# A fused tokenizer, attention and mixture-of-experts layer on one core: the last attention turn reordered, the first weight split on the vector engine, and one transpose per half group's maxima

## The reference, cut to what matters

```
h = concat([tok(x), txt], axis=1)                      # 8 x 384 x 256
# attention: 16 heads of 16, latent keys and values, causal softmax
n = layernorm(h);  c = n @ W_DKV                       # latent, 64
q, k, v = n @ W_UQ, c @ W_UK, c @ W_UV
h = h + softmax(causal(q k^T / 4)) v @ W_O
# experts: 8 of them, top 2, capacity 384 tokens each, first come first served per choice
n = layernorm(h);  s = softmax(n @ router_w);  w, e = top_k(s, 2)
for k in 0, 1:                                         # (choice, expert) = one unit
    y = gelu(xe @ w1[e]) @ w2[e]                       # xe: the rows sent to expert e, 384 x 256
    out[token] += w[:, k] * y
h = h + out + bias
```

## Time and profile before

| what | value |
| --- | --- |
| median of 3 runs | 673.88 us (670.34 to 673.93) |
| the profiled execution's own time | 673.71 us |
| its span, first to last instruction | 671.9 us |
| mean granted TensorE clock | 0.974 of 2.4 GHz |
| busy: TensorE, VectorE, ScalarE, GpSimd | 617.8, 403.1, 378.0, 389.8 us |
| instructions | 13720 |

### The profile page before, as it was taken

The page is one execution under the profiler, slowest core; times in us unless marked ns, Lnnn a source line. Parts: engine busy times, 40 slices in busy tenths (PEclk is TensorE's granted clock), DMA queues, the critical chain, the costliest instruction groups (busy, mean ns, idle before and its releaser), DMA issues.

```text
span 671.9 us, 13720 instructions
## 1 busy us (share of the span) xinstructions
PE 617.8 (92%) x5082; PEld 512.7 (76%) x5082; DVE 403.1 (60%) x942; ACT 378.0 (56%) x818; POOL 389.8 (58%) x600
## 2 busy tenths in 40 slices
PE   2698999999999999999879799999999999999992
PEld 2465566676666666666559699999999999999992
DVE  4778688788998888678446244544444444444320
ACT  4347786777776776666551355455445555455440
POOL 3303232424645555464655579998888888888223
PEclk9988999999999999999978799999999999999997
DMA  6527566633534232360111743554444444442123
GB/s 225 156 57 185 177 198 179 179 101 97 158 81 119 61 106 82 95 213 28 50 48 40 222 159 67 145 128 101 89 94 95 98 108 111 108 107 48 19 23 39
DMA packets 66604, 73.86 MB, mean 110 GB/s; under 512 B 6312, under 2 KB 61586, under 8 KB 66536
## 3 DMA queue, kind: packets, MB, share of 16 engines
q1 hardware_dynamic: 56232, 59.45, 29.7%
q0 software_dynamic: 9504, 13.00, 11.2%
q10 hardware_dynamic: 800, 0.52, 0.3%
HBM read 31.62 MB, written 22.48 MB: 81 GB/s over the span
## 4 chain that ended last, share of the span: by engine, by line
PE 82%; ACT 4%; DMA 4%; issue 3%; DVE 2%; SPq 1%; POOL 1%; ACTq 0%; another core or an unknown queue 0%; DVEq 0%; POOLq 0%
PE t_bank L1764 20%; PE bank L1779 14%; PE s_bank L1779 7%; PE bank L684 7%; PE t_bank L649 6%; PE s_bank L627 5%; PE t_bank L742 3%; PE s_bank L628 3%; PE t_bank L712 2%; PE s_bank L1749 2%; PE bank L696 2%; PE bank L754 1%; PE t_bank L727 1%; PE bank L775 1%; PE t_bank L747 1%
## 5 line engine op out<-in xcount | busy, mean ns | idle before, releaser
L1726 DVE TENSOR_TENSOR hl<-h,hh 128x384 fp32r<-128x384 f32 x128 | 108.1, 852 | 152.2 <-ACT h L1689 152.2
L550 POOL TENSOR_SCALAR_AFFINE_SELECT pt<-pt 128x256 f32<-128x256 f32 x192 | 83.9, 443 | 158.3 <-ACT pt L959 121.2
L1178 DVE TENSOR_REDUCE mx<-s_bank 128x2 f32<-128x256 f32 (+2 forms) x192 | 123.1, 683 | 47.7 <-PE s_bank L628 47.2
L1686 ACT ACTIVATE hh<-t_bank 128x384 fp32r<-128x384 f32 x128 | 63.0, 492 | 134.5 <-PE t_bank L1764 132.2
L1639 POOL DMA_INDIRECT out<-yo,xr x48 | 75.4, 1570 | 57.3 <-ACT yo L1697 47.3
L959 ACT ACTIVATE pt<-t_bank 128x512 f32<-128x512 f32 x128 | 76.0, 601 | 36.6 <-PE t_bank L649 34.8
L1626 POOL TENSOR_TENSOR wl<-wr,wh 128x256 fp32r<-128x256 f32 x112 | 95.2, 884 | 1.2
L1764 PE MATMUL t_bank<-xh,wh 128*128 128x384 f32 x256 | 87.2, 341 | 0.6 <-issue 0.6
L1764 PE MATMUL t_bank<-xl,wh 128*128 128x384 f32 x256 | 86.5, 338 | 0.0
L1764 PE MATMUL t_bank<-xh,wl 128*128 128x384 f32 x256 | 86.4, 338 | 0.0
L627 PE MATMUL s_bank<-ks,qs 96*128 96x128 bf16 (+2 forms) x384 | 80.2, 278 | 3.0 <-DMA qs<-part 2.8
(11 more groups left out here) (191 smaller groups left out, 1338.3 us busy)
## 6 DMA issues: line engine op xcount, KB each, us to landing
wr<-in_w SPq DMA_DIRECT2D x16, 1024.0 KB, 5.9
qs<-part SPq DMA_DIRECT2D x96, 96.0 KB, 2.2
ks<-part SPq DMA_DIRECT2D x90, 96.0 KB, 2.2
slot_rows<-empty SPq DMA_DIRECT2D x4, 1560.0 KB, 8.9
xr<-slot_rows SPq DMA_DIRECT2D x16, 390.0 KB, 3.3
wr<-in_x SPq DMA_DIRECT2D x8, 768.0 KB, 5.5
out<-hid SPq DMA_DIRECT2D x8, 384.0 KB
qs<-mT ACTq DMA_DIRECT2D x64, 3.0 KB
```

What stands on the lines that cost most here:

```text
L550: pool.affine_select(out=blocks, in_=blocks, compare_op=ALU.is_ge, fill=0.0, base=0, pattern=[[0, 2], [1, P]], channel_multiplier=-1).then ...
L1178: ins = dve.tensor_reduce(mx[:, p // 2, j, 2 * (p % 2):2 * (p % 2) + 2], pair_region(s_bank, j), AX_X, ALU.max)
L1726: dve.tensor_tensor(hl[:, f, :], h[f % 2][:, :], hh[:, f, :].bitcast(F32), ALU.subtract).then_inc(hl_done, 1)
```

## The change

- `maxima` on TensorE: the order of `mx`, `ms` and `mT` is changed so that one transpose of 24 columns (part, head, tile) replaces the three. ACT copies 24 x 128 instead of 8 x 384. Each of the two DMAs reads 12 partitions of 128 values instead of 4 of 384. The two DMAs of turn 15's second half group are issued by SP, the others by ACT as before.
- TensorE's list for turn 15 and the tail has another order. Before: contexts_back(14, 1), project(6, 0), ranks(5), then pair 2's groups. After: pair 2's groups and `values` follow at once, project(6, 0), ranks(5) and project(6, 1) stand among and behind pair 3's groups, project(7) comes ahead of rows_back(6), and there are more and longer fillers (6, 12, 6, 12, 24, 8, 24, 230 where 30, 20, 200 stood).
- ACT's list: contexts_out(14) after all exponentials, contexts_out(15) and `early_high` (now only w2) ahead of rows_back(6).
- VectorE's list: `weigh(5)` ahead, then a half of `early_first` (a copy to the high part and the subtraction for the low part of w1), the normalise of turn 15's first half group, the other half of `early_first`, and then residual and norm of entry 6. normalise(15, 1) ahead of the row scaling of entry 6. `early_low` and `late_bias` are gone from the end; the bias adds stand behind steps 1, 3 and 5 of the first expert unit.
- SP: the weights of expert 1 are loaded ahead of the stores of entries 5 to 7.

```
-    mx = buf("mx", [P, NG, NT, GH])
-    ms = buf("ms", [P, NG, NT, MPARTS, GH], BF16)
-    mT = buf("mT", [MPARTS * GH, NG, T], BF16)
+    mx = buf("mx", [P, NG, GH, NT])
+    ms = buf("ms", [P, NG, MPARTS, GH, NT], BF16)
+    mT = buf("mT", [MPARTS * GH * NT, NG, P], BF16)
...
+    def max_rows(queue, n, grp):
+        queue.wait_ge(mT_sb, NG * n + grp + 1)
+        for a in range(MPARTS):
+            queue.dma_start(qs[(n // 2) % 2][n % 2][MROW + a:MROW + a + 1, grp * GH:(grp + 1) * GH, :],
+                          mT[a * GH * NT:(a + 1) * GH * NT, grp, :]).then_inc(m_in[grp], 16)
...
+        max_rows(sp, END, 1)
...
-            for j in range(NT):
-                mm = pe.transpose(M_b[0:MPARTS * GH, j * P:(j + 1) * P],
-                                  ms[:, grp, j, :, :].rearrange("p a h -> p (a h)"), ident_b[:, :])
-            mm.then_inc(mT_ps, 1)
+            pe.transpose(M_b[0:MPARTS * GH * NT, 0:P], ms[:, grp, :, :, :].rearrange("p a h j -> p (a h j)"),
+                         ident_b[:, :]).then_inc(mT_ps, 1)
...
         contexts_back(END - 1, 1, False)
-        project(B - 2, 0)
-        ranks(B - 3)
         shifted_scores(END, 2, 0)
         shifted_scores(END, 2, 1)
         values(END, 0)
+        shifted_scores(END, 2, 2)
         contexts_out(END - 1, 0)
-        shifted_scores(END, 2, 2)
-        project(B - 2, 1)
         shifted_scores(END, 3, 0)
         contexts_back(END, 0, False)
         shifted_scores(END, 3, 1)
+        project(B - 2, 0)
         shifted_scores(END, 3, 2)
+        ranks(B - 3)
+        project(B - 2, 1)
         values(END, 1)
+        turning(6)
         contexts_back(END, 1, False)
+        turning(12)
+        contexts_out(END, 0)
+        turning(6)
+        for k in range(2):
+            project(B - 1, k)
         for c in range(KC):
             rows_back(B - 2, c)
-        contexts_out(END, 0)
-        for k in range(2):
-            project(B - 1, k)
+        turning(12)
         router(B - 2)
-        turning(30)
+        turning(24)
         for c in range(KC):
             rows_back(B - 1, c)
         ranks(B - 2)
+        turning(8)
         router(B - 1)
-        turning(20)
+        turning(24)
         ranks(B - 1)
-        turning(200)
+        turning(230)
...
-            act.activation(mT[:, grp, :], M_b[0:MPARTS * GH, 0:T], ACT.Copy).then_inc(mT_sb, 1)
+            act.activation(mT[:, grp, :], M_b[0:MPARTS * GH * NT, 0:P], ACT.Copy).then_inc(mT_sb, 1)
...
         exps(END, 0, 1)
-        max_rows(END, 1)
...
         contexts(END, 0)
-        contexts_out(END - 1, 0)
         exps(END, 2, 2)
         exps(END, 3, 0)
         exps(END, 3, 1)
         exps(END, 3, 2)
+        contexts_out(END - 1, 0)
         contexts(END, 1)
+        contexts_out(END, 0)
+        early_high(act)
         for c in range(KC):
             rows_back(B - 2, c)
-        contexts_out(END, 0)
-        early_high(act)
...
         reciprocals(END - 1, 1)
         normalise(END - 1, 1)
+        weigh(B - 3)
+        dve.wait_ge(t_ready, 12 * END)
+        early_first(dve, 0)
+        reciprocals(END, 0)
+        normalise(END, 0)
+        early_first(dve, 1)
         residual(B - 2, 0)
         norms2(B - 2, (0, 1))
-        weigh(B - 3)
-        reciprocals(END, 0)
-        normalise(END, 0)
         residual(B - 2, 1)
         norms2(B - 2, (2,))
         variances2(B - 2)
         keep_ranks(B - 3)
         place(B - 3)
-        scaled2(B - 2)
         reciprocals(END, 1)
         normalise(END, 1)
+        scaled2(B - 2)
...
-        early_low(dve)
-        for b in range(LATE, B):
-            late_bias(b)
...
+    BIAS_AT = (1, 3, 5)
...
         for u in range(1, NX):
             load_rows(u)
-        stores(sp)
         for i in range(2):
             load_weights(1, i)
+        stores(sp)
...
     def early_high(act):
 
-        for i in range(2):
-            act.wait_ge(w_in[i], 16)
-            for half in range(2):
-                cols = slice(half * NW // 2, (half + 1) * NW // 2)
-                act.activation(wh[i][0][:, cols], wr[i][:, cols], ACT.Copy).then_inc(w_first[i], 1)
-
-    def early_low(dve):
+        act.wait_ge(w_in[1], 16)
         for half in range(2):
             cols = slice(half * NW // 2, (half + 1) * NW // 2)
-            dve.wait_ge(w_first[0], half + 1)
-            dve.tensor_tensor(wl[0][0][:, cols], wr[0][:, cols], wh[0][0][:, cols].bitcast(F32),
-                              ALU.subtract).then_inc(w_split[0], 1)
+            act.activation(wh[1][0][:, cols], wr[1][:, cols], ACT.Copy).then_inc(w_first[1], 1)
+
+    def early_first(dve, half):
+
+        cols = slice(half * NW // 2, (half + 1) * NW // 2)
+        dve.wait_ge(w_in[0], 16)
+        dve.tensor_copy(wh[0][0][:, cols], wr[0][:, cols]).then_inc(w_first[0], 1)
+        dve.wait_ge(w_first[0], half + 1)
+        dve.tensor_tensor(wl[0][0][:, cols], wr[0][:, cols], wh[0][0][:, cols].bitcast(F32),
+                          ALU.subtract).then_inc(w_split[0], 1)
...
             hidden(0, f)
             if f == SECOND_AT:
                 rows(1)
+            if f in BIAS_AT:
+                biases(dve, BIAS_AT.index(f))
```

More of the change, by code:

```diff
@@ L74 @@
 NMAT = MAT_WO + KC * DIM + KC * E
-Programs = namedtuple("Programs", "sync gpsimd tensor scalar vector early_high early_low stores", defaults=(None,) * 3)
+Programs = namedtuple("Programs", "sync gpsimd tensor scalar vector early_high early_first stores biases", defaults=(None,) * 4)
 def rows_to_all(ap, n):
@@ L139, in _ @@
         def _(dve):
-            before.vector(dve, behind.early_low)
-            behind.vector(dve)
+            before.vector(dve, behind.early_first)
+            behind.vector(dve, before.biases)
 def front(nc, common, lent, wr, w_in, routed, x, txt, params, mats, w1, w2, slot_rows, out):
@@ L965, in maxima @@
                 act.wait_ge(m_in[grp], 16 * MPARTS * n)
-            act.activation(mT[:, grp, :], M_b[0:MPARTS * GH, 0:T], ACT.Copy).then_inc(mT_sb, 1)
-        def max_rows(n, grp):
-            act.wait_ge(mT_sb, NG * n + grp + 1)
-            for a in range(MPARTS):
-                act.dma_start(qs[(n // 2) % 2][n % 2][MROW + a:MROW + a + 1, grp * GH:(grp + 1) * GH, :],
-                              mT[a * GH:(a + 1) * GH, grp, :]).then_inc(m_in[grp], 16)
+            act.activation(mT[:, grp, :], M_b[0:MPARTS * GH * NT, 0:P], ACT.Copy).then_inc(mT_sb, 1)
         def contexts(n, grp):
@@ L1087, in scalar @@
                 if p == 0 and cur:
-                    max_rows(n, 1)
+                    max_rows(act, n, 1)
                 if p == 2 and nxt:
-                    max_rows(n + 1, 0)
+                    max_rows(act, n + 1, 0)
                 if not odd and p == 0 and live(b + 2) and n:
@@ L1163, in scalar, with late_bias, vector @@
         gates(B - 1)
-    def vector(dve, early_low):
+    def late_bias(dve, b):
+        dve.wait_ge(row_done, (NT + 1) * b + NT + 1)
+        dve.tensor_tensor(hid[:, b, :, :], hid[:, b, :, :],
+                          bias.rearrange("p (o d) -> p o d", o=1).to_broadcast([P, NT, DIM]),
+                          ALU.add).then_inc(res_last, 1)
+    def vector(dve, early_first):
         steps = [0]
@@ L1177, in maxima @@
             for j in BANK_TILES[grp]:
-                ins = dve.tensor_reduce(mx[:, p // 2, j, 2 * (p % 2):2 * (p % 2) + 2], pair_region(s_bank, j),
+                ins = dve.tensor_reduce(mx[:, p // 2, 2 * (p % 2):2 * (p % 2) + 2, j], pair_region(s_bank, j),
                                         AX_X, ALU.max)
@@ L1186, in split_high @@
                 dve.wait_ge(mT_ps, G - 1)
-            dve.tensor_copy(ms[:, grp, :, 0, :], mx[:, grp, :, :]).then_inc(m_part, 1)
+            dve.tensor_copy(ms[:, grp, 0, :, :], mx[:, grp, :, :]).then_inc(m_part, 1)
         def split_low(n, grp):
             dve.wait_ge(m_part, MPARTS * (NG * n + grp) + 1)
-            dve.tensor_tensor(ms[:, grp, :, 1, :], mx[:, grp, :, :], ms[:, grp, :, 0, :],
+            dve.tensor_tensor(ms[:, grp, 1, :, :], mx[:, grp, :, :], ms[:, grp, 0, :, :],
                               ALU.subtract).then_inc(m_part, 1)
@@ L1363, in keys @@
             dve.tensor_copy(part[k][stage][:, :], bank_of(part_key(b, k))[:, 0:T]).then_inc(part_dve, 1)
-        def late_bias(b):
-            dve.wait_ge(row_done, (NT + 1) * b + NT + 1)
-            dve.tensor_tensor(hid[:, b, :, :], hid[:, b, :, :],
-                              bias.rearrange("p (o d) -> p o d", o=1).to_broadcast([P, NT, DIM]),
-                              ALU.add).then_inc(res_last, 1)
         dve.wait_ge(prm_in, 16)
@@ L1499, in vector, with biases @@
         place(B - 1)
-        early_low(dve)
-        for b in range(LATE, B):
-            late_bias(b)
-    return Programs(sync, gpsimd, tensor, scalar, vector, stores=stores)
+    def biases(dve, b):
+        late_bias(dve, LATE + b)
+    return Programs(sync, gpsimd, tensor, scalar, vector, stores=stores, biases=biases)
 def s_region(bank, j, i):
```

(4 more changed lines are left out.)

## The result

The changed kernel takes 680.74 us (median of 8 runs, 678.07 to 682.34), the kernel before took 673.71 beside it (8 runs). The ratio is 1.0104, with a 95% interval of 1.0081 to 1.0126: slower by 1.0%, where 1.4% faster was forecast. The profiled execution took 682.34 us, span 680.6, at a mean granted clock of 0.967.

What follows compares the result with a forecast made beforehand. TensorE was taken to bound the steady attention turns and expert stage, a chain over all engines the stretch between. Terms: -3.5 - 2.3 + 0 - 1.8 - 1.9 + 0.2 = -9.3, so 673.7 becomes 664.4 us; range 659.8 to 669.0.

Steps and rivals of the forecast that it cites:

- Term 1: Attention turns: one transpose per half group instead of three, 32 half groups, -3.5 us (bounds -1.8 and -4.5).
- rival of late rows: Attention turns: maxima rows' DMA lands late, delaying each of 32 landings by 0.5 us; 680 us, chance 0.02.
- the transposes hide: Attention turns: dispatch around the transposes sets the pace, so they save only 0.5 us; 667.4 us, chance 0.05.
- Term 2: Last attention turn: new order starts values earlier and has the last rows transposed sooner, -2.3 us (bounds -0.8 and -3.7).
- the clock falls: TensorE's clock drops in the last turn or in the gap before the experts; 668.1 us, chance 0.17.
- Term 3: Ranks of the last batch: VectorE's remote wait stays, 0 us; bounds -1.7 and some 0.5 slower from low-clock fillers.
- Term 4: Last batch's sends: without VectorE's work beside them they shorten, so the row load starts earlier, -1.8 us.
- Term 5: Start of expert stage: 230 fillers nearly fill the wait, clock stays at 2.4 GHz, -1.9 us (bounds 0 and -2.6).
- Term 6: First expert unit: moved bias adds and later stores are covered by VectorE's idle time, +0.2 us (bound +1.5).
- the list of what would make it wrong: Signs, among them VectorE or ACT waits in the first expert unit idling TensorE, and waits for expert 1's split weights.

Runs made afterwards that it cites:

- h3: The change again, unedited, on a chip where the kernel before took 671.52 us: 679.01 us, ratio 1.0128.
- e1: The change with 110 instead of 230 products in its last filler: 670.78 us, ratio 0.9962 to the kernel before.
- e2: The change with its bias adds back at the end of VectorE's attention program: 672.58 us, ratio 0.9991 to the kernel before.
- e5: The change with 108 long fp32 instructions (0.22 us each) as last filler instead of 230 short products: 681.39 us, ratio 1.0112 to the kernel before.
- e6: The change without its last filler: 665.96 us, ratio 0.9886 to the kernel before.
- e7: The kernel before with the one transpose and one DMA for both maxima rows of a half group: 667.27 us, ratio 0.9916.
- h2: The kernel before with one transpose and one DMA for both maxima rows, repeated on another chip: 666.96 us, ratio 0.9918.
- e3: The kernel before with the one transpose alone, still two DMAs: 671.60 us, ratio 0.9959.
- g1: The change, unedited, on a chip where the kernel before took 661.95 us: 660.42 us, ratio 0.9964.
- g2: The kernel before, unedited, profiled on a chip where it took 661.95 us: 660.89 us, ratio 0.9984.
- e4: The kernel before with 230 instead of 200 products in its last filler: 674.09 us, ratio 1.0017.
- g3: The change without its last filler, on a chip where the kernel before took 661.95 us: 661.41 us, ratio 0.9975.
- h1: The change with 50 long products as last filler, bias adds moved, one maxima DMA, one projection reordered; kernel before 671.52 us: 664.51 us, ratio 0.9883.

## Why the prediction was wrong

**Term 1, −3.5: the mechanism was right, half the size.** The stretch from the 3rd to the 29th values holds 26 of the 32 half groups, so 2.9 us were due. On the 672 chips the six profiles with one transpose and two DMAs that keep the change's order (change, h3, e1, e2, e5, e6) lie between 238.2 and 239.6, against 240.2 and 240.3: about 1.4 less. With one DMA it is 237.8 and 237.9: 2.4 less. The step that failed is "with one wait of 0.2 us seen, I cost it at nothing". The transfer did cost nothing (one wait of 0.2 us, as before); its issue on ACT did not. A half group's two issues cost ACT 0.28 us more and its copy 0.21 us less. With half of the issues the kernel gained (e7 and h2: 0.9916 and 0.9918 against 0.9959 for e3), so ACT's time for issues is paid for there; that the 0.14 us alone are the missing half of term 1 is not shown, as e7 and h2 take away more than that. The rival of late rows fell. On the 660 chips the steady turns take 236.4 to 237.1 with any of the variants, so there term 1 is zero within what the profiles can tell. That is the rival "the transposes hide", for those chips.

**Term 2, −2.3: gave about nothing.** 29th values to last ranks: 39.6 and 39.0 before, 40.0 and 39.1 after, and 36.3 and 36.0 on the 660 chip. "The values start at about 331.5, 1.6 us earlier" can't be seen in the change's own profile: counted from the 29th values, the 31st start 14.0 us later in it and 13.9 before, and the last 20.1 and 20.2. The granted clock was low there from 322.3 to 329.1, which is half of the rival "the clock falls". But such a time differs from profile to profile by more than this term. In the six 672 profiles with the change's order the 31st come 12.3 to 14.0 us after the 29th, in the five with the old order 13.9 to 15.8; the means are 1.6 us apart, so this step held on the average. The step that failed is what follows them: from the end of the last values to the transposes of the last rows I had 12.2 us in the new order. In g1 it is 12.1, as worked out, but on that chip the old order needs only 10.1 (g2), so of the 2.3 us by which the last values ended earlier after the 29th, 2.0 were lost again behind them. In the profiles of the result it was 12.9 in the new order, 11.8 in the old. POOL was not late: the deviation was ready at 348.0, and VectorE then took up its logits at 348.14 after waiting 2.75 us for router 6. "What is late next is POOL's queue of sends, no longer TensorE" was wrong: it was TensorE.

**Term 3, 0: about right for the wait, not for the fillers.** The wait was 1.50 us against 1.71. It was 0.66 to 1.73 us in all twelve profiles on 672 chips and at most 0.31 in the eight on 660 chips, with either order, so it goes with the kind of chip. What I had kept as the bound on the other side, fillers at the low clock that hold up the last ranks by 0.5 us, came true: from the last rows' transposes to the last ranks it took 5.6 us instead of 5.0, and the 24 fillers between them 2.72 us. On the 660 chip it was 5.0 in both orders.

**Term 4, −1.8: right for the sends.** First to third send ended 3.53 us after the start of the first, where it was 5.39: −1.86. Both sides were seen on the 660 chip too: the old kernel has sends of 1.65, 1.70 and 1.44 us beside VectorE's weight split and bias adds, the new one 0.97. SP issues the row load at 364.21, not 371.03. That is 1.5 us more than the sends gave: the issue follows the end of the third send after 1.44 us, where it was 2.97. It is 1.4 us in e3 and e7 too, with the old order and the long sends, and 2.97 in e4, so this part is not from the shorter sends; I had not looked at it. By the rule of the Trainium skill (SBUF — State Buffer, Who interferes with whom) that a two-input `tensor_tensor` leaves descriptor writing alone, which the page marks as inferred, this would have been 0; the rows disagree.

**Term 5, −1.9: its second half was right, its first was the error.** From the transposes to the first result product the experts took 10.9 us, 2.2 less than before. What failed is "14.0 us are filled by 230, 13.1 to 13.6 us: a gap of about 0.5 to 1", on both sides. The 14.0 us were 11.8: e6 has the rows at 367.95, and the filler starts at 356.20. So 230 products would have held the experts up by 1.3 us even at their pace of 13.00 us (g1), and on the 660 chip they did: 13.1 us from the last ranks to the experts with the filler (g1), 11.1 without (g3). There it cost nothing in the end (660.42 us with the filler, 661.41 without), as without it the clock was low for 14 us. And on the 672 chip they did not keep that pace: it took 23.3 us from their start to the experts', which is 11.6 us behind the rows. A filler in front of a wait had been priced at its pace, with no price for its running over; taking it out gave 14.8 us, to 0.9886, which is 7.7 us under the kernel before on its chip.

**Term 6, +0.2: mis-sized through term 5.** The cover I named, VectorE's idle time in the first unit, was there only while GpSimd was not splitting weights. The loads of expert 1 did not wait for TensorE, so the splits came 14.9 us after the experts' start before, 11.0 in g1 and 2.7 in the change. Beside them a bias add took 1.49 instead of 0.90 us and `hl` 1.05 instead of 0.56, and TensorE waited 3.31 us and fell to the low clock (393.9 to 400.8). e2 prices it: 301.1 down to 294.8, so 6.3 us, or 4.6 against h3; in e2 the splits also begin 2.4 us later after the experts' start, so a part of this may be theirs. The text had put the danger into the list of what would make it wrong, but not into the range.

**The rivals.** None of them came out as a whole. The one on the slower side (DMA landing late) was the wrong mechanism; the right one, a filler that ends after the rows, was within sight: it needed only the question what happens if the 0.5 to 1 us of slack is not there.

**What the gaps are stays open.** Shown: on 672 chips they came in all five profiles in which the short products ran further than 1.5 us beyond SP's issue of the first row load (the change, e1, e2, e4, h3), and not in e3, e7 and h2, whose 200 products ended 1.3 to 1.5 us after it; they begin after 85, 89, 114, 173 and 217 products (e1, h3, the change, e2, e4); short products show them and long ones do not (e5, h1). The timeline of SP beside them, over two windows:

```profile
364.21 9.05 SPq L1597 DMA_DIRECT2D xr<-slot_rows  x4
```

```profile
364.21 0.39 SPq L1597 DMA_DIRECT2D xr<-slot_rows  x1
```

The first row is four issues of 0.37 to 0.49 us merged into one, not one issue of 9 us. Behind the first of them the program has SP wait for GpSimd's last six sends, and issues the other three from 371.83 on. The end of the gaps goes with the end of that wait: 372.15 in the change, 369.0 in h3 (SP goes on at 368.80), 372.7 in e2 (372.98), 373.7 in e4 (373.79). Their start goes with nothing that I found. It lies 1.1 to 1.4 us ahead of the first issue in the change, h3 and e1, so that issue can't have begun them there, and 1.0 to 1.2 us behind it in e2 and e4. The last packet of instructions that the traces show before the gaps starts 1.5 to 6.3 us ahead of them, which is no fixed distance either.

Nor is TensorE alone late in this stretch. In e3 its transposes ended at 371.64, but ACT, which had nothing else to do, took up their first half, ready before that, at 373.81:

```profile
370.30 1.34 PE L1747 MATMUL s_bank<-ident,xr 128*128 128x128 f32 x6 [2.65 <-DMA xr<-slot_rows]
...
373.81 0.87 ACT L1679 ACTIVATE xh<-s_bank 128x384 fp32r<-128x384 f32 x2 [17.59 <-remote]
```

From the start of the transposes to that copy it took 3.51 us here, 2.06 in e7 and 1.65 in h1, and 0.54 in the change and in g1, where the transposes came after the stretch or on a 660 chip. With VectorE's wait for the ranks (term 3) that makes three engines that are late on the 672 chips alone.

In the kernel before, the first row load was issued at 371.03, just after the 200 products had ended at 370.84: TensorE then waited anyway. By this the change brought its own loss about, as term 4 drew the issue under the filler and the longer filler reached further behind it; that is argued from the order of events. In g1 the filler runs 6 us beyond the first issue (357.97) without a gap. A supply of instructions that falls behind on some chips, or a slower hand-over between engines while the sends and SP's wait last, are guesses; no run moved the sends or the row loads to test either.

## What to carry to other kernels

A filler that stands in front of a wait is not free: price the case that it outlasts the wait, and size it by the earliest end of the wait and not by the latest; here it decided the sign. When a start is late, look at what does not move with it: loads and splits that go on at their own time land beside other work. And run both kernels on several chips before a gain or loss of 1% is called one of the code.

## What the runs showed of the hardware

- The same program took 671.5 to 673.7 us on some chips and 659.9 to 662.0 on others. By the table 3.8 us of the 13.1 lie in the steady turns, 3.3 in the last turn, 2.7 between ranks and experts, 2.7 before the third values (of which up to 2.9 also vary on one chip) and 0.7 in the expert stage, where TensorE has products of 0.3 us.
- Runs of short products (0.056 us each) stalled on the 672 chips with nothing to wait for that the profile shows: 24 of them took 9 us. On the same chips VectorE took up finished ranks late (waits of 0.66 to 1.73 us, at most 0.31 on the 660 chips).
- The issue of a DMA on ACT took 0.58 us for one row from 4 partitions, 0.72 for one row from 12, and 0.62 for two rows from 24.
- One row of a timeline can merge issues with a wait between them: four issues of 0.37 to 0.49 us read as one of 9.05.
- Where VectorE worked without a break beside GpSimd's weight splits, both were slower: two `hl` took 2.10 us, and GpSimd's eight subtractions 9.17 in the change against 6.82 in e2. With breaks, as in e2, single `hl` beside the same subtractions took 0.56 to 0.86.
